# Key choice of the first two batches beside the last early tiles; the second batch's QKV copied by ScalarE; routed sums behind the last maximum

## The reference

```python
x = x + haar_attention(LN(x))                     # "a"
x = x + moe(LN(x), Wg, W1, W2)                    # "g": 8 experts, the best 2 of each token
x = x + sparse_attention(LN(x), Wq, Wk, Wv, Ws)   # "c" and the 16 groups
x = x + moe(LN(x), Wg, W1, W2)                    # "t": the same experts again

# sparse attention, 16 heads of 8 channels:
scores  = (x @ Ws.T + bs).transpose(0, 2, 1)
top_idx = top_k(scores, 128)                      # for each head its own 128 of 512 keys
out = (local_band(q, k, v) + softmax(q @ k[top_idx].T) @ v[top_idx]
       + softmax(q @ k[:64].T) @ v[:64]) / 3
```

## Time and profile before

| | us |
|---|---|
| median of 3 runs | 568.15 (567.2 to 568.41) |
| the profiled execution | 569.34 |
| its span | 567.5 |
| PE busy in the span | 497.0 (88%) |
| DVE, ACT, POOL busy | 390.0, 350.9, 311.3 |

### The profile page before, as it was taken

One profiled execution on the slowest core, in us unless ns is written; L12 is line 12 of the kernel. 1 busy time (PEld: TensorE's weight loads), 2 busy tenths in 40 slices (PEclk: granted clock), 3 DMA queues, 4 the chain that ended last, 5 costly groups with the idle time before them and its releaser, 6 DMA issues.

```text
span 567.5 us, 13117 instructions
## 1 busy us (share of the span) xinstructions
PE 497.0 (88%) x4267; PEld 307.3 (54%) x4267; DVE 390.0 (69%) x1400; ACT 350.9 (62%) x835; POOL 311.3 (55%) x464
## 2 busy tenths in 40 slices
PE   7999899886767999999899989899987878789886
PEld 4477676676434445545455545445544422668664
DVE  4777876468886698899878897777975650235325
ACT  6587555786208676667567668566664455567653
POOL 3411165456499976493199967897075051354340
PEclk9999999998989999999999999999999697999999
DMA  7996011764210000000000000010001005356506
GB/s 229 360 362 228 2 42 56 255 206 156 64 29 14 3 14 14 14 4 15 12 9 9 15 12 14 27 30 20 12 4 45 12 34 183 125 183 195 163 15 185
DMA packets 47539, 47.78 MB, mean 84 GB/s; under 512 B 10323, under 2 KB 39129, under 8 KB 47472
## 3 DMA queue, kind: packets, MB, share of 16 engines
q1 hardware_dynamic: 44464, 41.37, 23.2%
q0 software_dynamic: 3008, 5.58, 3.1%
HBM read 11.32 MB, written 19.48 MB: 54 GB/s over the span
## 4 chain that ended last, share of the span: by engine, by line
PE 58%; DVE 17%; issue 9%; ACT 7%; DMA 3%; POOL 3%; another core or an unknown queue 2%; SPq 1%; DVEq 0%; ACTq 0%; POOLq 0%
PE BANK L1836 5%; PE BANK L1935 5%; PE BANK L1912 4%; PE BANK L1804 4%; PE BANK L1792 4%; PE BANK L1884 4%; PE BANK L2022 4%; PE BANK L1941 2%; PE BANK L1938 2%; PE BANK L2160 2%; PE BANK L1741 2%; PE BANK L1907 2%; POOL OH L725 2%; DVE XN_c L1460 2%
## 5 line engine op out<-in xcount | busy, mean ns | idle before, releaser
L1117 ACT ACTIVATE PT<-BANK 128x256 f32<-128x256 f32 (+2 forms) x352 | 158.1, 493 | 108.5 <-PE BANK L1912 75.1
L725 POOL TENSOR_SCALAR OH<-IOTA,POS 128x128 bf16<-128x128 bf16 x240 | 140.1, 604 | 4.3 <-DVE OH L1580 3.2
L1460 DVE CUSTOM_DVE_ANT_0 XN_a<-BANK,BANDQ 128x256 f32<-128x256 f32 (+1 forms) x128 | 56.7, 443 | 25.6 <-PE BANK L1884 15.6
L1460 DVE CUSTOM_DVE_ANT_0 XN_c<-BANK,BANDQ 128x384 f32<-128x384 f32 (+1 forms) x128 | 67.9, 530 | 9.3 <-PE BANK L1884 5.5
L733 POOL TENSOR_TENSOR SUM<-NRM 128x128 f32<-128x128 f32 x16 | 7.3, 456 | 104.5 <-DVE NRM L1481 104.5
L1465 DVE TENSOR_REDUCE QST<-BANK 128x4 f16<-128x512 f32 x64 | 44.2, 694 | 16.8 <-PE BANK L1889 12.7
L1935 PE MATMUL BANK<-PT,V 128*32 128x256 f32 (+1 forms) x512 | 49.1, 456 | 0.7 <-issue 0.3
L757 POOL DMA_INDIRECT yt_late<-QKV,IDY_late x31 | 30.4, 979 | 32.7 <-DVE QKV L1338 25.2
L1836 PE MATMUL BANK<-XNT_ALL,W 128*128 128x512 f32 x96 | 45.3, 596 | 0.0
L934 ACT ACTIVATE PT<-BANK 128x512 f32<-128x512 f32 x48 | 27.6, 598 | 22.3 <-PE BANK L1836 20.4
L1907 PE MATMUL BANK<-BANDK,IDB 128*128 128x256 bf16 x128 | 36.0, 282 | 5.7 <-issue 3.5
(11 more groups left out here) (363 smaller groups left out, 1286.6 us busy)
## 6 DMA issues: line engine op xcount, KB each, us to landing
xs_late<-W SPq DMA_DIRECT2D x1, 6984.0 KB, 38.4
xs_early<-W SPq DMA_DIRECT2D x1, 4680.0 KB, 19.6
KZB<-W SPq DMA_DIRECT2D x16, 256.0 KB
KZC<-W SPq DMA_DIRECT2D x15, 256.0 KB
PT<-W SPq DMA_DIRECT2D x11, 256.0 KB
QKV<-xs_late SPq DMA_DIRECT2D x31, 72.0 KB
W<-w SPq DMA_DIRECT2D x2, 1024.0 KB, 8.5
QKV<-xs_early SPq DMA_DIRECT2D x23, 72.0 KB
```

The source lines that it names most:

```text
L725: last = nc.gpsimd.tensor_scalar(OH[g % 2][:, i, t, :], IOTA[:, :], POS[:, t, c:c + 1], None, ALU.is_equal)
L1117: nc.scalar.activation(PT[u % PT_RING][:, 0:w], P2_BANK[u % SCORE_RING][:, 0:w], ACT.Exp, scale=SCALE).then_inc(S["exp_done"], 1)
L1460: nc.vector.tensor_tensor_reduce(out=JUNK[v % 2][:, 0:n], in0=P1_BANK[v % SCORE_RING][:, 0:n], in1=BANDQ[:, off:off + n], scale=1.0, scala ...
```

## The change

- PE turns the mask behind tile 20 into MISC (`MARKS_TILE`) and counts the places behind tile 21 (`PLACES_TILE`) into bank 0, where the tiles' turns went. DVE does its part of both, and group 0's one-hot matrices, ahead of maximum 0 and no longer between the maxima.
- `c_turn(1)` and the scores stand one tile earlier (tiles 1 and 2). Row numbers are written for four tiles by one instruction (`early_ids`), with 2, 6, 8, 8 and 8 half rounds behind the first five of the six calls.
- The second batch's QKV products leave tiles 7 to 11: two stand between the last tile and unit 0, three behind units 5, 8 and 11. ACT copies them out of PSUM (`one_stored`), DVE adds the bias at units 7, 8, 9, 11 and 12 of group 0 (`one_bias`), and ACT's `stack_first_parts(1)` goes from unit 8 to unit 14.
- `gather_kv(0)` stands behind unit 2; all 22 maxima follow, then the routed sums and statistics, then the first four maxima of group 1. Most `keep_busy` products go.
- In group 0, `gather_kv(2)` goes from unit 13 to unit 19, and batch 2's and 3's norms from units 4 and 7 to 7 and 11. Group 2's units keep the plain order (`q_unit`). POOL does `rstd("c", 1)` ahead of `stacks(0)`.

```diff
-    if g >= 2:
+    if g >= 3:
         return Q_ORDER[w]
-C_TILE, SCORES_TILE, QKV_TILE, QK_TILE, VALUE_TILE = 2, 3, 7, {5: 0, 6: 1}, 4
-ROUNDS_TILE = {i: 1 + (i + 1) % 2 if i < 13 else 2 for i in range(4, NT_EARLY - 1)}
+C_TILE, SCORES_TILE, MARKS_TILE, PLACES_TILE, QK_TILE, VALUE_TILE = 1, 2, 20, 21, {5: 0, 6: 1}, 4
+ID_TILES = 4
+ROUNDS_ID = {0: 2, 4: 6, 8: 8, 12: 8, 16: 8}
+BIAS_ONE = {(0, 7): 0, (0, 8): 1, (0, 9): 2, (0, 11): 3, (0, 12): T}
+STACK_ONE = (0, 14)
-NORMS_C = {(0, 4): 2, (0, 7): 3}
+NORMS_C = {(0, 7): 2, (0, 11): 3}
...
+            def early_ids(first):
+                tiles = range(first, min(first + ID_TILES, NT_EARLY))
+                for n in tiles:
+                    dve.wait_ge(TILE_IN["early"][n % IN_RING], 32 * (n // IN_RING + 1))
+                lo = first % IN_RING
+                nc.vector.tensor_scalar(IDY["early"][:, first:first + len(tiles)], ROW_IN[:, lo:lo + len(tiles), D + 1], float(UNUSED), None,
+                                        ALU.add).then_inc(R["early"]["tile_id"], len(tiles))
...  (DVE)
-            for i in range(NT_EARLY):
-                early_id(i)
-                if QKV_TILE <= i < QKV_TILE + T + 1:
-                    c_add(1, i - QKV_TILE)
-                rounds(0, ROUNDS_TILE.get(i, 0))
-            rounds(0, 2 * ROUNDS - taken[0])
+            for first in range(0, NT_EARLY - ID_TILES, ID_TILES):
+                early_ids(first)
+                rounds(0, ROUNDS_ID[first])
             mask(0)
-            maxima(range(0, 3))
+            early_ids(NT_EARLY - NT_EARLY % ID_TILES)
             dve.wait_ge(S["sel_t"], 1)
-            marks(BANK[0]).then_inc(S["sel_t_s"], 1)
-            maxima(range(3, 7))
+            marks(MISC).then_inc(S["sel_t_s"], 1)
             dve.wait_ge(S["sel_pos"], 1)
             places(0, PLACE_BANK).then_inc(S["sel_done"], 1)
...
-            maxima(range(7, 10))
+            maxima(range(0, 3))
             gathered_kv(0)
+            maxima(range(3, UNITS_Q))
             for a in range(EARLY.first, B):
                 add_experts(EARLY, a)
                 dve.wait_ge(S["x_sum"], a - EARLY.first + 1)
                 stats("c", a)
-            maxima(range(10, UNITS_Q))
             maxima(range(UNITS_Q, UNITS_Q + FIRST_LEAD))
...  (PE)
+                if i == MARKS_TILE:
+                    pe.wait_ge(S["misc_free"], free("qk", 1) + 1)
+                    pe.wait_ge(S["sel_mask"], 1)
+                    sel_marks(MISC).then_inc(S["sel_t"], 1)
+                if i == PLACES_TILE:
+                    pe.wait_ge(R["early"]["tile_xt"], NT_EARLY)
+                    pe.wait_ge(S["sel_t_s"], 1)
+                    sel_places(PLACE_BANK).then_inc(S["sel_pos"], 1)
...
+            c_qkv(1, 0)
+            c_qkv(1, 1)
             pe.wait_ge(R["early"]["tile_y"], NT_EARLY)
             for w in range(0, 3):
                 p1(0, w)
-            keep_busy(IDLE_BANK, 6)
-            pe.wait_ge(S["sel_mask"], 1)
-            sel_marks(BANK[0]).then_inc(S["sel_t"], 1)
...
+            gather_kv(0)
+            for w in range(3, UNITS_Q):
                 p1(0, w)
-                keep_busy(IDLE_BANK, 1)
+                if w in (5, 8, 11):
+                    c_qkv(1, (w + 1) // 3)
+                else:
+                    keep_busy(IDLE_BANK, 1)
             keep_busy(IDLE_BANK, 4)
+            pe.wait_ge(S["c_stored"], 2 * (T + 1))
             transpose_again(0)
             for w in range(FIRST_LEAD):
                 p1(1, w)
```

## The result

| | before | after |
|---|---|---|
| median of 5 runs each, same chip | 568.38 (567.2 to 572.07) | 571.37 (571.05 to 573.84) |
| profiled execution | 569.34 | 571.05 |
| its span | 567.5 | 569.2 |

The ratio is 1.0074, 95% interval 1.0041 to 1.0107: the change made the kernel slower by about 0.7%. 566.85 was predicted, with 564.0 to 570.8 as its range, and 571.37 was measured.

The account below looks back on a forecast made before the run. It took DVE's list to bound the lead-in and PE the later groups. Start of group 0 -0.5, clock +0.8, group 0 -1.6 made -1.3 us: 566.85 for the median, range 564.0 to 570.8.

Parts of the forecast that it names:

- (1): Early tiles: without QKV products in tiles 7 to 11 the tile stage ends 1.5 us earlier.
- (6): Group 0: dividing ACT's norms and casts shortens it; from -3.0 to +1.0 us, taken as -1.6.
- (7): Groups behind group 0: no change expected; one changing its length by over 0.5 us would prove the prediction wrong.
- the sums take the place, on a cold PE: Rival, lead-in and group 0: tile stage ends no earlier, two half-clock stretches follow; +2.7 us, 570.85; chance 0.24.
- the lock: Rival, end of tiles: DVE's one-hot matrices hold up POOL's last scatters by up to 2.7 us; 568.85; chance 0.08.
- (2): Last tiles: mask at 140 to 142, ahead of tile 20; products and copies cost 0.25; last result about 145.7.
- (3): DVE's list behind the tiles: one-hot matrices from 145.7, about 3 us idle before the chosen keys, last maxima done 163.5.
- (4): End of lead-in: the sums' 5.5 us stay on the path; PE's first unit of group 0 at 169.6, 0.5 earlier.
- (5): Start of group 0: PE's idle time brings a clock of 0.5 on the first units, costing 0.8 us.

Follow-up runs that it names:

- e2: Changed kernel with 20 idle products on PE under the routed sums, ahead of group 1's unit 3; 1.0057 of the kernel before.
- e0_after: Changed kernel, unedited, run and traced on a quiet chip (kernel before takes 542 us there); 1.0065 of the kernel before.
- e8: Changed kernel with only group 2's gather back at unit 13 of group 0; 1.0042 of the kernel before.
- e10: Changed kernel with e9's edits, but sums behind maximum 17 and SP spreading group 0's chosen keys before group 1's keys; 0.9877 of the kernel before.
- g1: e10 run again on a chip where the kernel before takes 572 us; 0.9944 of the kernel before.
- e11: e10 with 13 more idle products on PE while DVE does the sums; 0.9889 of the kernel before.
- b0_before: Kernel before, unedited, run and traced on a quiet chip (542 us there); ratio 0.9995.
- e14: Changed kernel with only the first gather's wait cut loose from POOL's wait for the last scatters; 1.0072 of the kernel before.
- f2: Kernel before with sums behind maximum 17 instead of 9 and SP spreading group 0's chosen keys before group 1's keys; 1.0004 of the kernel before.
- e9: Changed kernel with POOL's old order, group 2's old order, its gather at 13, sums behind maximum 9, first gather's own wait; 0.9970 of the kernel before.
- f3: Changed kernel with group 2's gather at 13, its old order and sums behind maximum 17; 1.0045 of the kernel before, 1.0024 when run again.
- f1: Changed kernel with two idle products on PE after each of tiles 7 to 11; 1.0069 of the kernel before.
- e1: Changed kernel with POOL's stacks again ahead of the second batch's norms, as before; 1.0057 of the kernel before.

## Why the prediction was wrong, step by step

The forecast was wrong in sign: -1.3 us was foreseen, +3.0 measured between the medians. Three of its steps failed. The last result was to come 1.25 earlier and came 0.4 later, since the swap on POOL's list, which the sum left out, held DVE's norms up (1). Group 0 was to give back 1.6. Dividing ACT's norms and casts gave nothing, and `gather_kv(2)`, put between two other users of its bank, cost 1.1 net (6). And the groups behind were put at nothing and lost 0.8 and, by a code fetch, 1.2 (6, 7).

Of the rivals the one called *the sums take the place, on a cold PE* came true almost to the tenth in the lead-in: results readable 151.5 said, 151.8 measured (first issue of the reads); chosen keys 162.0, 162.1; end of the last maximum 164.7, 165.0; sums 170.2, 170.2; PE's first unit 170.8, 170.84. Its time, 570.85, is 0.5 short, and that is partly luck. It put two stretches of half clock at +2.5 and group 0 at -0.5; one such stretch cost 1.07 (e2), and the losses at units 19 and 20 and in groups 1 and 5 stand in no rival. Nor was its reason right: the tile stage did get shorter, but it started later.

(1) *QKV out of the tiles, 1.5 earlier.* The size was right, the result wasn't. From POOL's first scatter to its last the stage takes 40.66 us instead of 41.75 on the first chip (108.84 to 149.50, before 107.20 to 148.95), and 36.33 instead of 37.70 on the quiet one. But it starts 1.64 later, since DVE's four norms take 2.81 instead of 1.12 beside POOL's stacks and the row numbers stand behind them. The prediction named the lock, looked for it at the one-hot matrices and gave it 0.08. There it costs nearly nothing: the last two scatters take 1.02 instead of 0.97. It missed that the swap on POOL's list, which it didn't cost at all, makes the same pair of engines meet at tile 1. The second of ACT's results shows how much: it comes 1.20 behind the first in the kernel before, 3.35 in e0_after and e8, and 2.10 in e10 and 2.09 in g1, which have POOL's old order. So 1.25 is the swap and 0.9 the turn of the normed rows at tile 1 instead of 2, where PE waits for them. With the swap undone and no half clock there (e10, e11), the way from the norms to the last scatter is 1.2 to 1.3 shorter than in b0_before, about what the prediction had foreseen; b0_before has a stretch of half clock from 139.6, to which a part of that may be due. PE in e0_after:

```profile
107.00 0.66 PE L1764 MATMUL BANK<-IDENT,XN_c 128*128 128x128 f32 x4 [1.04 <-DVE XN_c L1227]
```

Nor is PE what ends the stage. On the quiet chip POOL issues 16 scatters from 121.06 on, about 1.28 apart, with three value parts between and no gap over 0.8, so products taken off PE bring little there. The last of them in e0_after:

```profile
141.65 0.97 POOL L767 DMA_INDIRECT yt_early<-QKV,IDY_early  x1 [0.30 <-issue]
142.93 0.97 POOL L767 DMA_INDIRECT yt_early<-QKV,IDY_early  x1 [0.30 <-issue]
144.21 0.97 POOL L767 DMA_INDIRECT yt_early<-QKV,IDY_early  x1 [0.30 <-issue]
```

(2) *Mask at 140 to 142, ahead of tile 20.* Right: it is written from 138.96. The last result at 145.7: wrong, 147.30, the second of the two in this row of ACT, with marks and places standing among the last tiles of a PE that pauses on this chip (DVE waits 5.58 for the marks):

```profile
147.04 0.63 ACT L1000 ACTIVATE QKV<-BANK,QKV 128x128 f32<-128x128 f32 x2 [1.75 <-remote]
```

(3) *The one-hot matrices at 145.7, DVE idle 3 us ahead of the chosen keys.* The structure is right, the chosen keys gate. The gap is 0.57, because 2.08 us more stand further up, at the first gather: the wait for `stack_v` behind POOL's wait for the scatters, which the prediction overlooked. By e14 it alone costs nothing, as SP's chain is longer.

(4) *169.6 for the first unit.* 170.84. The sums' own length, 5.3 for 5.5, was right. The error comes down SP's chain from (1): the reads of the results start 1.9 later than foreseen, the four maxima on the chosen keys 1.5.

(5) *The clock, 0.8.* A stretch at 0.50 lies there, 169.1 to 175.9, and costs 1.07 (e2). The mechanism was right, the size a little short.

(6) *Group 0, -1.6.* Its mechanism failed. Units 8 to 18 take 9.9 us instead of 12.1 on the first chip, but none of that comes from dividing the norms and casts. 1.3 of it is unit 13, which takes 2.74 in the stretch of low clock of the earlier trace rows and 1.41 in b0_before; neither b0_before nor f2, the other traces with the old group 0, has that stretch. The rest is the gather that has left unit 13. With the gather back there (e8) units 8 to 18 take 11.3 us, against 10.8 in b0_before. Unit 8 falls from 2.63 to 0.57, but units 11 and 14, where the second norm and the casts stand now, rise from 0.37 and 0.39 to 1.91 and 2.35. With the gather at 13, group 2's old order and a full clock group 0 takes 23.1 (e9, e11, f3), with the old places 22.6 (b0_before, f2). Not foreseen were 2.5 us at units 19 and 20, where 1.4 at unit 13 would have been the price at the old place. The prediction asked for that gather only whether POOL would be ready, and not which bank it uses and who else uses it there. It cost the plain order of group 2 at 0 to 0.5; that is 0.8, in group 1.

(7) *Later groups unchanged.* More than 0.5 in one of them was named as a sign of being wrong. Group 5 is 2.7 longer. 1.2 of it is PE's wait for the chosen keys of group 6. The changed kernel, PE at the start of group 5:

```profile
273.11 0.38 PE L1924 MATMUL BANK<-QS,QT 128*128 128x128 f16 x4 [1.08 <-DMA HXT<-KALL]
```

SP had issued the last of them at 269.15, 4.0 us before PE can go on. In e0_after 3.8 us pass from that issue to the landing, in b0_before 1.7. In between a piece of program code was fetched. Transfers of e0_after in the 1.7 us from 265.6 on (GB/s in 40 slices; q8 is the fetching of instructions):

```profile
GB/s 6 79 49 30 404 0 0 0 0 0 0 0 0 0 0 0 0 0 0 0 0 0 0 0 0 0 0 0 0 0 0 0 0 0 0 6 6 0 0 0
DMA packets 49, 0.02 MB, mean 14 GB/s; under 512 B 48, under 2 KB 48, under 8 KB 48
## 3 DMA queue, kind: packets, MB, share of 16 engines
q8 instruction: 1, 0.02, 4.9%
```

45 of the 48 packets go through, then the fetch, and the last three start 1.3 us later, as it ends. In all fifteen traces in which the fetch falls between these packets the last three are late by 0.8 to 1.3, and unit 0 of group 5 takes 1.58 to 2.08. In the five in which it comes earlier (before, b0_before, f1, f2) or just after the last packet (e9) it takes 0.83 to 0.99. f1 is the changed kernel with ten products more ahead of that point. So the change lost this 1.2 by the place at which a fetch falls. The other 1.5 goes with a stretch of half clock from 281.7, at unit 9 of that group. Nine of the eighteen traces of the experiments have one there, e0_after has not, and f2, a version of the kernel before, has. With a trace or two of each kernel it can't be told whether the change makes it more frequent; that stays open.

Where the sum stands, in the profiled executions of the first chip: predicted -0.5 for the start, measured +0.9; -0.8 for clock and group 0 together, measured +1.2; nothing for the rest, measured +0.8, +2.7 and -3.9.

Open: how much of the first chip's 0.74% is each place's, since its pauses differ from run to run, and whether the place of marks and places in the last tiles costs anything there. Not tried, since it isn't free of races: POOL's copies for the global values ahead of its wait for the scatters.

## What to carry to other kernels

A step that is moved has three addresses: the engine's list, the buffer that it shares, and the semaphore that it waits on. Ask at the new place who uses the buffer just before and after, and what stands ahead of the instruction that sets the semaphore. Where a transfer gates the end of a lead-in, put the work that needs none of it right in front of the wait, and not behind it. And price a swap of two small steps on GpSimd by what runs on VectorE at that moment.

## What the runs showed of the hardware that I had not expected

- Four VectorE instructions between SBUF tiles take 1.12 us alone and 2.81 when the first two run beside GpSimd's two tensor_tensor between SBUF tiles (e1 and e0_after). GpSimd's take 1.15 each in both.
- With a fetch of 16 KB of program code between them, the last three packets of a transfer of 8 KB come 0.8 to 1.3 us late, in fifteen traces of fifteen. Some of SP's issues are longer too: 0.59 is usual, and the one below took 1.46 in e0_after. All seven issues over 0.8 us among its 160 for keys have a fetch beside them, though other issues beside a fetch keep their length.

```profile
153.58 1.46 SPq L570 DMA_DIRECT2D PR<-KALL  x1
```

- The same program takes 542 us on two chips and 568 to 572 on three others. Of the 30.7 us between the spans of before and b0_before, 19.6 are PE standing still (70.5 against 50.9), up to 3.1 us at a time with no wait to show, above all in the tiles and behind group 5. The other 11.1 are PE busy for longer (497.0 against 485.9), at a mean granted clock of 0.974 against 0.993.
